# A query's reciprocal length as the scale of the exponential, a clamp by a pair maximum, and a later place for two deviations

## The reference

```
def l2norm(t):
    return t / jnp.maximum(jnp.linalg.norm(t, axis=-1, keepdims=True), 1e-12)
...
def attn_layer(x, Wqkv, qs, ksc, Wo):          # 16 heads of 64, windows of 32
    q, k, v = heads of x @ Wqkv
    q = l2norm(q) * qs
    k = l2norm(k) * ksc
    q = q * cos * scale + rotate_half(q) * sin * scale
    k = k * cos * inv + rotate_half(k) * sin * inv
    out = local_attention(q, k, v)             # a window sees itself and the one before
    return out @ Wo
...
def local_attention(q, k, v):
    sim = einsum(q, k) * 8, masked
    attn = jax.nn.softmax(sim, -1)
    return einsum(attn, v)
...
for i in range(6):
    x = attn_layer(shift_tokens(x), ...) + x
    x = ffn_layer(shift_tokens(x), ...) + x
```

## Time and profile before

| what | value |
|---|---|
| median of 3 runs | 2578.75 us (2575.7 to 2585.78) |
| the profiled execution's own time | 2579.93 us |
| its span, first to last instruction | 2578.1 us |
| TensorE, VectorE | 92%, 88% of the span busy |
| GpSimd, ScalarE | 75%, 72% busy |
| mean granted clock of TensorE | 0.98 |

### The profile page before, as it was taken

How to read it: one execution, slowest core, us unless ns; L and a number is a source line. 1 busy time by engine, 2 the same in 40 slices (tenths; PEclk the granted TensorE clock), 3 DMA queues, 4 the chain that set the end, 5 groups by cost and what they waited for, 6 DMA issues and landing times. The chain is left out here.

```text
span 2578.1 us, 67512 instructions
## 1 busy us (share of the span) xinstructions
PE 2359.5 (92%) x26742; PEld 1421.1 (55%) x26742; DVE 2272.9 (88%) x2520; ACT 1848.5 (72%) x4093; POOL 1944.9 (75%) x1768
## 2 busy tenths in 40 slices
PE   7999999899898879899899999999999999999997
PEld 4444443333333346566566666666666666666665
DVE  6778879879999988999678999899999999899994
ACT  4566555556666647787678888788888888888883
POOL 2441147947889857777578999799998999899991
PEclk9999999999999989999899999999999999999999
DMA  3000000003232310300212121112211121111101
GB/s 109 9 9 11 9 7 7 20 20 56 58 59 58 59 33 8 98 15 12 66 47 43 31 59 39 37 33 47 49 43 29 40 63 33 35 35 33 30 17 40
DMA packets 171111, 97.22 MB, mean 38 GB/s; under 512 B 97155, under 2 KB 167791, under 8 KB 169263
## 3 DMA queue, kind: packets, MB, share of 16 engines
q1 hardware_dynamic: 170799, 92.91, 15.8%
HBM read 66.91 MB, written 7.08 MB: 29 GB/s over the span
## 5 line engine op out<-in xcount | busy, mean ns | idle before, releaser
L608 PE MATMUL ps<-xnT,qp 128*128 128x512 f32 (+3 forms) x1280 | 562.3, 560 | 11.1 <-ACT prob L833 11.0
L833 ACT ACTIVATE prob<-ps,mneg,shift 128x1024 f32<-128x1024 f32 (+7 forms) x384 | 366.2, 954 | 285.5 <-DVE mneg L728 285.1
L1924 DVE TENSOR_TENSOR area<-ps,tab 128x2048 f32<-128x2048 f32 x192 | 430.5, 2283 | 66.1 <-ACT area L1710 38.7
L728 DVE TENSOR_REDUCE mneg<-ps 128x1 f32<-128x1024 f32 (+7 forms) x384 | 340.0, 886 | 73.7 <-PE ps L608 73.3
L1441 PE MATMUL ps<-wqk,area 128*128 128x512 f32 x768 | 357.2, 607 | 28.0 <-DVE area L1990 23.1
L736 DVE STREAM_TRANSPOSE area<-prob 128x1024 f32<-128x1024 f32 (+7 forms) x384 | 351.5, 916 | 31.1 <-ACT prob L833 24.9
L2111 POOL TENSOR_TENSOR area<-area,rn 128x1024 f32<-128x1024 f32 x192 | 370.5, 1950 | 7.5
L1531 PEld LDWEIGHTS ps<-wvo,area 128*128 128x128 f32 x3072 | 352.9, 192 | 26.1 <-issue 20.9
L1531 PE MATMUL ps<-wvo,area 128*128 128x128 f32 x3072 | 359.6, 275 | 3.3 <-ACT area L1759 3.3
L608 PEld LDWEIGHTS ps<-xnT,qp 128*128 128x128 f32 x1280 | 222.3, 196 | 202.2 <-issue 174.3
L1752 ACT ACTIVATE ps<-ps,nmxl 128x64 f32<-128x64 f32 x1536 | 321.3, 343 | 5.7 <-DVE nmxl L1904 5.5
(11 more groups left out here) (276 smaller groups left out, 4351.2 us busy)
## 6 DMA issues: line engine op xcount, KB each, us to landing
xe<-bc_scratch SPq DMA_DIRECT2D x128, 128.0 KB, 3.7
area<-bc_scratch SPq DMA_DIRECT2D x128, 128.0 KB, 4.0
staged<-values_scratch SPq DMA_DIRECT2D x192, 32.0 KB, 1.9
wqk<-lwqk_dram SPq DMA_DIRECT2D x6, 1024.0 KB, 6.4
xp<-xc SPq DMA_DIRECT2D x96, 48.0 KB, 2.8
xc<-xs SPq DMA_DIRECT2D x96, 32.0 KB
wvT<-lwvT_dram SPq DMA_DIRECT2D x6, 512.0 KB, 8.0
wo<-lwo_dram SPq DMA_DIRECT2D x6, 512.0 KB, 10.2
```

What stands on the lines that cost most here:

```text
L608: mm = E.matmul(ps[:, r + o // 512, 0:w], k.qp[:, group % 2, i * P:(i + 1) * P], k.xnT[:, k0 + o:k0 + o + w], start=o // 512 != masked, st ...
L728: V.tensor_reduce(k.mneg[:, U:U + 1], of, X_AXIS, ALU.max, negate=True).then_inc(s("top"), 1)
L833: A.activation(k.prob[:, U % 2, 0:nk], ps[:, r:r + 2, :].rearrange("p a b -> p (a b)")[:, 0:nk], ACT.Exp, bias=k.mneg[:, U:U + 1], scale=k ...
L1924: V.tensor_tensor(k.rot[:, n % 2, w, :, :].rearrange("p c (h d) -> p c h d", d=DH), bcast(heads(what, n), 1, 2), bcast(k.tab[:, n % FRAME, ...
```

## The change

There are three parts.

1. *The query's reciprocal length.* GpSimd's product for q goes; `normal` becomes `normal_keys`. `turn_rows` of q waits for `add` alone. The scores then lack the query's factor. `top` multiplies the negated maximum by `rn` in a second VectorE instruction, 128x16, with a wait for its own first one; the exponential gets `rn` of its token and head as its scale operand. The order of the heads differs between `nmxl` (parity first) and `rn`, hence the rearrangements.
2. *The clamp.* `ss` becomes pairs; the second of each pair is filled with 1e-24 once. The sums go to the first, with a stride of two, and the clamp is a maximum over each pair, a `tensor_reduce` in the place of a `tensor_scalar`.
3. *The deviations* and two small copies of step 0 move behind the `add` of tile 2.

```
     def turn_rows(what, n):
...
-        E.wait_ge(s("normal_" + what), n + 1)
+        E.wait_ge(s("added_q" if what == "q" else "normal_k"), n + 1)
...
     def probs(n, o):
...
-            ins = A.activation(here, here, ACT.Exp, bias=k.nmxl[:, n % 2, 8 * o + j:8 * o + j + 1])
+            ins = A.activation(here, here, ACT.Exp, bias=k.nmxl[:, n % 2, 8 * o + j:8 * o + j + 1], scale=k.rn[:, n % 2, 2 * j + o:2 * j + o + 1])
...
     def top(n):
         V.wait_ge(s("lscore"), n + 1)
-        V.tensor_reduce(k.nmxl[:, n % 2, :], heads("scores", n), X_AXIS, ALU.max, negate=True).then_inc(s("top_s"), 1)
+        V.tensor_reduce(k.nmxl[:, n % 2, :], heads("scores", n), X_AXIS, ALU.max, negate=True).then_inc(s("v"), k.v.up())
+        V.wait_ge(s("v"), k.v.n)
+        V.wait_ge(s("rn_better"), n + 1)
+        here = k.nmxl[:, n % 2, :].rearrange("p (o j) -> p o j", o=2)
+        V.tensor_tensor(here, here, k.rn[:, n % 2, 0:H].rearrange("p (j o) -> p o j", o=2), ALU.mult).then_inc(s("top_s"), 1)
...
     def sum_squares(n):
...
-        V.tensor_reduce(k.ss[:], k.sq.rearrange("p w (h d) -> p (w h) d", d=DH), X_AXIS, ALU.add).then_inc(s("summed"), 1)
+        V.tensor_reduce(k.ss[:, :, 0], k.sq.rearrange("p w (h d) -> p (w h) d", d=DH), X_AXIS, ALU.add).then_inc(s("summed"), 1)
...
-        V.tensor_scalar(k.sx[:, n % 2, :], k.ss[:], 1e-24, None, ALU.max).then_inc(s("squares"), 1)
+        V.tensor_reduce(k.sx[:, n % 2, :], k.ss[:], X_AXIS, ALU.max).then_inc(s("squares"), 1)
...
-    def normal(what, n):
-        w = 0 if what == "q" else 1
-        of = k.rot[:, n % 2, w, 0, :].rearrange("p (h d) -> p h d", d=DH)
+    def normal_keys(n):
+        of = k.rot[:, n % 2, 1, 0, :].rearrange("p (h d) -> p h d", d=DH)
         G.wait_ge(s("rn_better"), n + 1)
-        G.wait_ge(s("added_" + what), n + 1)
-        G.tensor_tensor(of, of, bcast(k.rn[:, n % 2, H * w:H * (w + 1)], 2, DH), ALU.mult).then_inc(s("normal_" + what), 1)
+        G.wait_ge(s("added_k"), n + 1)
+        G.tensor_tensor(of, of, bcast(k.rn[:, n % 2, H:2 * H], 2, DH), ALU.mult).then_inc(s("normal_k"), 1)
...
+    G.memset(k.ss[:], 1e-24)
...
     for n in range(LAST_STEP):
         if n + 1 < NTILE:
             better(n + 1)
-            normal("q", n + 1)
-            normal("k", n + 1)
+            normal_keys(n + 1)
...
-        if n == 0:
-            deviations()
-            for a in range(ET):
-                ins = G.tensor_copy(k.mxp[a][:, 0:PAD], k.tail[:, a, :])
-            ins.then_inc(s("padded"), 1)
...
         if n + 2 < NTILE:
             add("q", n + 2)
             add("k", n + 2)
+        if n == 0:
+            deviations()
+            for a in range(ET):
+                ins = G.tensor_copy(k.mxp[a][:, 0:PAD], k.tail[:, a, :])
+            ins.then_inc(s("padded"), 1)
```

More of the change, by code:

```diff
@@ L2159, in transformer_pool @@
     better(0)
-    normal("q", 0)
-    normal("k", 0)
+    normal_keys(0)
     add("q", 1)
@@ L2310, in build @@
             k.ln256 = sb("ln256", [P, 1], c=c)
-            k.ss, k.sx, k.rn, k.rt, k.lnx = sb("ss", [P, 2 * H], c=c), sb("sx", [P, 2, 2 * H], c=c), sb("rn", [P, 2, 2 * H], c=c), sb("rt", [P, 2 * H], c=c), sb("lnx", [P, 2 * H], c=c)
+            k.ss, k.sx, k.rn, k.rt, k.lnx = sb("ss", [P, 2 * H, 2], c=c), sb("sx", [P, 2, 2 * H], c=c), sb("rn", [P, 2, 2 * H], c=c), sb("rt", [P, 2 * H], c=c), sb("lnx", [P, 2 * H], c=c)
             k.kT = sb("kT", [P, 2, 8, KW], c=c)
```

## The result

The changed kernel takes 2675.93 us (median of 4 runs, 2675.01 to 2684.46) beside 2577.42 for the kernel before: ratio 1.0379, 95% interval 1.0363 to 1.0394. It is slower by 98 us. The direction and the main mechanism, longer exponentials on the path, were as forecast; the size was not: 2643 with a range up to 2670 was too low.

What follows compares the result with a forecast made beforehand. It took a loop of waits through VectorE, TensorE and ScalarE's exponentials as the bound, GpSimd outside it. Tiles +44, +15, +5, the maximum's product +6 and GpSimd -6 made +64 on the median 2578.75: 2643 us, range 2592 to 2670.

Steps and rivals of the forecast that it cites:

- The exponentials' second operand: ScalarE's 16 exponentials per tile, reading a scale column too, take 1.45 us more than 3.35; bounds 1.1 and 1.6.
- Rival A: The scale read of the 64-column exponentials is hidden, so the changed kernel is faster, 2555 us; chance 13%.
- the layers' starts: Tiles outside the first 22 and 52 ordinary ones: TensorE trails VectorE by more than the change adds, so only +5 us.
- the first 22 tiles: Opening tiles, where convolution and rate steps leave TensorE or GpSimd late: +0.68 us each, +15 us.
- The 44 us for ordinary tiles: 52 ordinary tiles: addition 1.36 us, clamp saving 0.40, TensorE's lead 0.11 in the mean; +0.85 each.
- the rule: Per tile: exponentials' 1.45 us, less the gap before `suml`, `sx`'s saving on the path, and TensorE's lead where late.
- The clamp: `sx` on VectorE as pair maximum stops waiting for GpSimd: 0.18 us, saving 0.42 per tile, 40 at most in all.
- the tiles' +0.85: Net cost in us of each of 52 ordinary tiles: longer exponentials less clamp saving and TensorE's lead.
- The product (+6): VectorE's multiplication of the maximum by `rn` may wait for GpSimd, mostly covered by the loop: +6 us, from 0 to +24.
- rival C: The maximum's multiplication waits for GpSimd on the path, 0.8 us in 40 tiles more: +32 us, 2675; chance 7%.
- GpSimd (-6, "it does not drive it"): GpSimd follows close behind the loop; losing 96 query products, with `deviations` moved, returns 6 us, from 0 to 16.
- the +64: Forecast total slowdown in us: tiles +44, +15 and +5, the maximum's multiplication +6, GpSimd -6; giving 2643.

## Why the prediction was right in its sign and wrong in its size

**The exponentials' second operand (forecast 1.45 us a tile): right.** 4.80 us in the row shown, 461.3 us in all. The price read off pairs at 512 columns held at 64: the starts of neighbours lie 0.29 us apart instead of 0.20. Rival A fell with it. The Trainium skill's figure (ScalarE: Activation LUTs, What ACT_TABLE_LOAD costs), 93 ns for each pointer operand, agrees with the trace.

**What it costs in the sum: mis-sized.** The failed step is "In the other tiles, at the layers' starts, where TensorE trails VectorE by more than the change adds, +5". It measured 22 us. TensorE trailed there, but not by its own work: it waited for a copy behind the exponentials in ScalarE's order, 17.2 us in ten waits already in the kernel before, eight of them in these groups. The row stood in the table of waits that I had before me; I took "late" as slack without asking what it was late for. The run without the column in these tiles and two ordinary ones brings 20 to 22 us back.

The step before it, the first 22 tiles at +15, measured 24 to 28; which waits make that difference no run separates, and two executions of the same code differ by 6.7 us there at tile 23.

The 44 us for ordinary tiles measured 49.5, and that it came so near was luck. The second column alone gave 51 us in these tiles where the rule made 65, and the clamp alone gave 7 back where it made 21: the two errors are of equal size, and they cancel.

**The clamp (0.42 us a tile, 40 us at most, and 30 of them on the path): its own time right, its worth wrong.** 0.22 us instead of 0.18 and no waits; but it is worth 11 to 12 us, alone as in the change. In the sum it was netted into the tiles' +0.85, and so hidden. Alone, TensorE's waits for GpSimd grew by 7 us beside it, and four tiles lost 1.4 to 2.1 us at a lower clock. In the change the old clamp would no longer have taken 0.60 us but 0.38, the mean of the run without the pair maximum, so that there was less to save.

**The product (+6): right.** 7 to 8 us above a reduce of 0.17 us in its place. It waits for GpSimd as L1147 had shown, in the median tile for 1.4 us of its 1.54, and the cover was there as the earlier trace rows said: ScalarE's waits for `nmxl` rose only to 16.5 us. The price of rival C was right for the instruction and its place wrong; that its 2675 is the measured time to a microsecond is chance, since the product makes 7 to 8 us of it and not 32. By the Trainium skill (SBUF — State Buffer, Who interferes with whom) an instruction with two inputs in SBUF contends with a GpSimd instruction that reads SBUF, and `tensor_reduce` does not contend. The trace agrees on both: 174 to 1884 ns for L1908, 219 to 222 for L1938.

**GpSimd (-6, "it does not drive it"): wrong for the kernel before, nearly right for the sum.** Without its products the kernel before gains 24 us, behind the longer exponentials 1 or 2. I had read the 24.1 us of the earlier trace rows as pairs of waits that something else would have caused anyway; with GpSimd busy 95 of 100 us they were a bound of their own. Without the products that row falls by 15 us, and the old clamp, which waits for GpSimd's instructions, takes 15 us less. The forecast of -6 was not saved by its reasoning but by the change itself, which moved the bound to ScalarE.

**The sum from the runs.** Second column +107, product +7, clamp -11, the deviations 0, GpSimd's products -1 to -2: +101 to +102, beside the +98 measured. What the +64 lacked: about 17 at the layers' starts, some 9 in the first tiles, where executions differ by up to 6.7, 5 in the ordinary ones; the clamp and GpSimd's part are inside these. Of the signs that the prediction named, the gaps before `suml` summed to 75 us and not 100, and GpSimd's idle time before its lengths grew as said.

**Which version is best.** The clamp's pair maximum without the rest: 2566 us, 0.3 to 0.6% below the kernel before and 4% below the change. To take GpSimd's product away is worth 24 us more, if the factor can be put somewhere that adds nothing to ScalarE's exponentials or to VectorE between `ss` and the projection. The factor could go to ScalarE's copy of the queries only if it were one number per partition there, and the copy stands behind the transpose, where it is not. No version with the factor kept and the product gone was found that is faster.

## What to carry to other kernels

A per-partition operand on a short activation is not free because the engine is 72% busy: sixteen times 0.09 us on the path cost more than 187 us of GpSimd's work off it gave back. When a tile looks late by another engine's own work, ask for that engine's waits there by line before counting the lateness as slack; an in-order engine passes a delay on to everything queued behind it, here to a copy that stands eight instructions later. And price a gain against every engine that is nearly full: where two bounds take turns, lifting one gives back only its own share. A term that nets a cost against a saving hides both: forecast them apart, and test them apart.

## What the runs showed of the hardware

- A 128x16 product of two SBUF tiles took 0.17 us at best and 1.54 in the median; of the 76 that took over 0.3 us, 74 ended within 0.1 us of the end of a GpSimd product. A reduce of 128x64 to 128x32 on the same engine never took more than 0.222 us.
- Four 512-column matmuls took 1.95 to 1.98 us at the full clock, and 3.44 where the window's granted clock was 0.83 and a wait of 1.80 us stood in front. But waits of equal length, 2.04 us, were followed by 1.95 us in one tile and 3.05 in another of the same kernel.
- A second column operand put the starts of neighbouring 64-column exponentials 0.29 us apart instead of 0.20.
- Two exponentials of 512 columns take 1.23 us where sixteen of 64 take 3.35, and 4.80 with a second column operand.
